# The first mixture's products in three fp32r parts, with split weights kept in DRAM and two smaller weight rings

## What is computed

```python
def _expert(xf, w1, w3, w2):
    return jax.nn.silu(xf @ w1) * (xf @ w3) @ w2
# D = 256, H = 128; routed_w1, routed_w3: (8, D, H), routed_w2: (8, H, D); shared_w*: the same for 2
```

## Time and profile before

| | us |
|---|---|
| median of 3 runs | 4491.06 (4484.61 to 4496.41) |
| the profiled execution, its own time | 4493.15 |
| its span, first to last instruction | 4491.3 |
| TensorE busy | 4192.4 (93%) |
| VectorE busy | 2936.4 (65%) |
| ScalarE busy | 2086.3 (46%) |
| mean granted TensorE clock | 0.973 of full |
| DRAM traffic | 202.34 MB read, 20.97 MB written |

### The profile page before, as it was taken

How to read it: one execution, slowest core, us unless ns; L and a number is a source line. 1 busy time by engine, 2 the same in 40 slices (tenths; PEclk the granted TensorE clock), 3 DMA queues, 4 the chain that set the end, 5 groups by cost and what they waited for, 6 DMA issues and landing times.

```text
span 4491.3 us, 73765 instructions
## 1 busy us (share of the span) xinstructions
PE 4192.4 (93%) x28256; PEld 3197.8 (71%) x28256; DVE 2936.4 (65%) x7633; ACT 2086.3 (46%) x3424; POOL 112.0 (2%) x196
## 2 busy tenths in 40 slices
PE   7898998989989899898999989999999999999998
PEld 4675966759667596675966759667696676956768
DVE  7567776676656666666665667657676576665655
ACT  4544455353553435535355353553535535356342
POOL 0000000000000000000000000000000000000000
PEclk8999999999999999999999999999999999999999
DMA  2010600103001030010300103001030010300112
GB/s 99 1 45 10 219 35 1 54 20 132 29 15 41 27 125 29 15 41 29 123 29 15 41 29 123 29 15 41 29 123 29 15 41 37 115 29 15 31 54 102
DMA packets 51768, 228.05 MB, mean 51 GB/s; under 512 B 4832, under 2 KB 21216, under 8 KB 31584
## 3 DMA queue, kind: packets, MB, share of 16 engines
q1 hardware_dynamic: 51424, 223.33, 13.8%
HBM read 202.34 MB, written 20.97 MB: 50 GB/s over the span
## 4 chain that ended last, share of the span: by engine, by line
PE 81%; DVE 11%; ACT 5%; issue 3%; DMA 0%; SPq 0%; DVEq 0%; ACTq 0%
PE w L574 18%; PE w L584 13%; PE o L709 11%; PE w L830 8%; PE w L820 8%; PE w L642 4%; PE w L558 4%; PE o L702 3%; DVE mx L1227 3%; PE w L625 3%; PE w L677 2%; PE w L567 2%; PE w L721 1%; PE w L612 1%; ACT pt_spread L975 1%
## 5 line engine op out<-in xcount | busy, mean ns | idle before, releaser
L1227 DVE TENSOR_REDUCE mx<-w 128x4 f32<-128x1024 f32 x512 | 606.8, 1221 | 181.4 <-PE w L625 168.4
L975 ACT ACTIVATE pt_spread<-w 128x1024 f32<-128x1024 f32 x512 | 520.2, 1024 | 235.5 <-PE w L642 202.9
L709 PE MATMUL o<-pt_spread,va 128*32 128x256 f32 x4096 | 540.9, 395 | 29.3 <-ACT pt_spread L975 28.6
L921 ACT ACTIVATE oth<-w,res 128x256 f32<-128x256 f32 x656 | 277.4, 472 | 574.6 <-PE w L820 469.8
L574 PE MATMUL w<-xnT,stream 128*128 128x256 f32 x1792 | 413.1, 382 | 1.4 <-ACT xnT L913 0.8
L574 PEld LDWEIGHTS w<-xnT,stream 128*128 128x128 f32 x1792 | 338.1, 191 | 50.8 <-DVE x L1196 1.0
L709 PEld LDWEIGHTS o<-pt_spread,va 128*32 128x32 f32 x4096 | 204.8, 111 | 200.0 <-issue 60.8
L820 PE MATMUL w<-qodd,va_hi 128*128 128x256 f32 x2048 | 344.9, 283 | 0.9 <-issue 0.6
L820 PEld LDWEIGHTS w<-qodd,va_hi 128*128 128x128 f32 x2048 | 284.6, 188 | 7.6 <-issue 2.3
L1483 DVE TENSOR_REDUCE mx<-w 128x2 f32<-128x1024 f32 x128 | 155.8, 1225 | 199.6 <-PE w L679 199.1
L1196 DVE SCALAR_TENSOR_TENSOR x<-w,gate,x 128x256 f32<-128x256 f32 x512 | 223.2, 477 | 89.8 <-PE w L830 71.7
(11 more groups left out here) (255 smaller groups left out, 7741.9 us busy)
## 6 DMA issues: line engine op xcount, KB each, us to landing
stream_lo<-split SPq DMA_DIRECT2D x56, 1024.0 KB, 4.8
va_hi<-split SPq DMA_DIRECT2D x56, 1024.0 KB, 6.9
stream<-in_moe_dram SPq DMA_DIRECT2D x80, 384.0 KB, 3.2
stream<-in_resident_dram SPq DMA_DIRECT2D x8, 2048.0 KB, 7.4
raw<-in_moe_dram SPq DMA_DIRECT2D x8, 1024.0 KB, 6.8
split<-va_hi SPq DMA_DIRECT2D x8, 1024.0 KB, 8.9
split<-stream_lo SPq DMA_DIRECT2D x8, 1024.0 KB, 10.9
stream<-in_resident_dram SPq DMA_DIRECT2D x8, 1024.0 KB, 4.7
```

The source lines that it names most:

```text
L709: mm = pe.matmul(o[g:g + 32, 0:T], by_heads(plan, s)[:, kt, plan.v_of(h), :], p[:, a * 512 + kt * T:a * 512 + (kt + 1) * T], start=(kt == ...
L921: h = act.activation(dst[:, c, :], w[:, c * T:(c + 1) * T], func, bias=bias[:, c:c + 1], **more)
L975: act.activation(exp_buffer(plan.name + ".exp", s, u), w[:, :], ACT.Exp, scale=scale).then_inc(S["s_P"], 1)
L1227: dve.tensor_reduce(mx[s][:, :, 2 * v:2 * v + 2].rearrange("p t a -> p a t"), w[:, :].rearrange("p (a t k) -> p a t k", a=2, t=TT), AX_X, ...
```

## The change

**Products.** f1's products become three fp32r products each. `f1.up` waits for the split activations of the element (`f1.xs`, new: VectorE copies `xnT` to a high part in `qodd` and subtracts for the low part) and issues 12 instead of 4; `f1.down` issues 6 instead of 2. The hidden activations are split too: after `f1.mul` ScalarE copies the product to a high part, and a new step `f1.part` on VectorE subtracts it for the low part; both lie in `ob_hi`.

**Weights.** In the first pass each expert's raw weights are loaded into the place of the low part and split by a new step `f1.split` (ScalarE: two copies, 512 and 256 columns; VectorE: two subtractions). SP writes both parts to DRAM (`split_up1`, `split_down1`), and in the seven later passes loads them split. Split weights take twice the room, so the ring of five becomes a ring of three for the up weights (1024 columns each, 512 KB) and a ring of two for the down weights (512 columns each, 256 KB): `RINGU`, `RINGD`. A load waits for both slots' `f1.up` of e-3 or `f1.down` of e-2, and in the first pass also for the write of what lay there. The loads of f2's first low parts wait for the last uses of the new regions.

**Order.** The new steps are put in, and the string `ORDER` is another one, so steps that the change doesn't name stand in another order as well.

```diff
 MOE1, MOE1_ROUTED, MOE1_COLS = 10, 8, 2 * 128 + 2 * 128 + 256
-RING1, RING2 = STREAM_COLS // MOE1_COLS, 2
+UP1_COLS, DOWN1_COLS = 2 * 512, 2 * 256
+RINGU, RINGD, RING2 = 3, 2, 2
+DOWN1_AT = RINGU * UP1_COLS
...
@@ -173,7 +175,7 @@
 def experts(n, s, count):
-    return [(f"{n}.{what}", s, e) for e in range(count) for what in ("up", "mul" if n == "f1" else "part", "down", "sum")]
+    return [(f"{n}.{what}", s, e) for e in range(count) for what in (("up", "mul", "part", "down", "sum") if n == "f1" else ("up", "part", "down", "sum"))]
...
@@ -184,7 +186,7 @@
-        + steps_of(s, "l2.init", "l1.oT", "l1.out", "f1.ln", "f1.xT", "f1.lg", "f1.gate") + experts("f1", s, MOE1)
+        + steps_of(s, "l2.init", "l1.oT", "l1.out", "f1.ln", "f1.xT", "f1.xs", "f1.lg", "f1.gate") + experts("f1", s, MOE1)
...
@@ -226,52 +228,54 @@
-        + [[x for x in every if x[0] == "l1.max"] + [("f2.split", s, e) for e in range(MOE2) if s == 0]]
+        + [[x for x in every if x[0] == "l1.max"] + [("f1.split", s, e) for e in range(MOE1) if s == 0] + [("f2.split", s, e) for e in range(MOE2) if s == 0]]
...
 ORDER = (
...
-    "DAM11ADM11ADDAAMAAAA7AAAJAMAAAAAAAMA1AMMAMAD0M050M50M505M0M50M50M50M5M0550M50M50M5M0M505M0M55CC5HC0HCHCHCHCHC2H0CH0CHHC0"
...
+    "DAM11ADM11ADDAAMAAAA7AAAJAMAAAAAAAMA1AMMAMAD0M050M50M505M0M50M50M50M5M0550M50M50M5MM0505M0M55CC5HCHCHCHCH0CHCHCH0CH0H0CH"
...
+        split_up1 = nc.dram_tensor("split_up1", (MOE1, P, UP1_COLS), F32, kind="Internal").ap()
+        split_down1 = nc.dram_tensor("split_down1", (MOE1, P, DOWN1_COLS), F32, kind="Internal").ap()
...
 
-        def expert1(e):
-            w = stream[:, e % RING1 * MOE1_COLS:(e % RING1 + 1) * MOE1_COLS]
-            return (w[:, 0:256].rearrange("p (k n) -> p k n", k=FC), w[:, 256:512].rearrange("p (k n) -> p k n", k=FC),
-                    w[:, 512:768].rearrange("p (k n) -> p k n", k=1))
+        def up1(e, buf):
+
+            w = buf[:, e % RINGU * UP1_COLS:(e % RINGU + 1) * UP1_COLS]
+            return w[:, 0:512], w[:, 512:1024]
+
+        def down1(e, buf):
+            o = DOWN1_AT + e % RINGD * DOWN1_COLS
+            return buf[:, o:o + 256], buf[:, o + 256:o + 512]
+
+        def loads1(p, e, ring):
+
...
@@ -771,18 +787,34 @@
 
             def ffn_1(what, s, e):
-                w1, w3, w2 = expert1(e)
                 w = take("f1." + what, s, e)
                 if what == "lg":
                     pe.wait_ge(*after("s_xnT", "f1.xT", s))
                     filled(by_tokens(w, xnT[s], mat("r1_w", FC), 8, FC))
                 elif what == "up":
-                    pe.wait_ge(S[f"s_moe1_{e % RING1}"], 16 * (pass_of(s) * len(range(e % RING1, MOE1, RING1)) + e // RING1 + 1))
-                    by_features(w, w1, xnT[s], 0, 1)
-                    filled(by_features(w, w3, xnT[s], 0, 1, T))
+                    if pass_of(s):
+                        pe.wait_ge(S[f"s_moe1_{e % RINGU}"], loads1(pass_of(s), e, RINGU))
+                    else:
+                        pe.wait_ge(*after("s_wl1", "f1.split", 0, e))
+                    pe.wait_ge(*after("s_xs", "f1.xs", s))
+                    hi, lo = (p.rearrange("p (j k n) -> p j k n", j=2, k=FC) for p in up1(e, stream_lo))
+                    xhi, xlo = qodd[s][:, 0:2, :], qodd[s][:, 2:4, :]
+                    for j in range(2):
+                        parts = [(wt, a, k) for wt, a in ((hi, xhi), (lo, xhi), (hi, xlo)) for k in range(FC)]
+                        for n, (wt, a, k) in enumerate(parts):
+                            mm = pe.matmul(w[:, j * T:(j + 1) * T], wt[:, j, k, :], a[:, k, :], start=(n == 0), stop=(n == len(parts) - 1))
+                    filled(mm)
                 else:
-                    pe.wait_ge(*after("s_up1", "f1.mul", s, e))
-                    filled(by_tokens(w, oth[s][:, 2 * (e % 2) + 1:2 * (e % 2) + 2, :], w2, D, 1))
+                    if pass_of(s):
+                        pe.wait_ge(S[f"s_moed_{e % RINGD}"], loads1(pass_of(s), e, RINGD))
+                    pe.wait_ge(*after("s_up1", "f1.part", s, e))
+                    hi, lo = down1(e, stream_lo)
+                    ahi, alo = (ob_hi[s][:, 2 * (e % 2) + n, :] for n in range(2))
+                    for tt in range(TT):
+                        parts = ((ahi, hi), (alo, hi), (ahi, lo))
+                        for n, (a, wt) in enumerate(parts):
+                            mm = pe.matmul(w[:, tt * D:(tt + 1) * D], a[:, tt * P:(tt + 1) * P], wt, start=(n == 0), stop=(n == len(parts) - 1))
+                    filled(mm)
...
@@ -1076,9 +1108,19 @@
                     w = full(act, step, s, u)
                     if u > 1:
-                        act.wait_ge(*after("s_up1", "f1.mul", s, u - 2))
+                        act.wait_ge(*after("s_mul", "f1.mul", s, u - 2))
                     act.activation(oth[s][:, 2 * (u % 2), :], w[:, 0:T], ACT.Silu).then_inc(S["s_silu"], 1)
 
+                elif step == "f1.mul":
+                    if u > 1:
+                        full(act, "f1.down", s, u - 2)
+                    act.wait_ge(*after("s_mul", step, s, u))
+                    act.activation(ob_hi[s][:, 2 * (u % 2), :], oth[s][:, 2 * (u % 2) + 1, :], ACT.Copy).then_inc(S["s_h1hi"], 1)
+                elif step == "f1.split":
+                    act.wait_ge(S[f"s_moe1_{u % RINGU}"], loads1(0, u, RINGU))
+                    act.wait_ge(S[f"s_moed_{u % RINGD}"], loads1(0, u, RINGD))
+                    act.activation(up1(u, stream_lo)[0], up1(u, stream)[1], ACT.Copy)
+                    act.activation(down1(u, stream_lo)[0], down1(u, stream)[1], ACT.Copy).then_inc(S["s_wh1"], 1)
                 elif step == "f2.split":
                     if u < 2:
...
@@ -1495,8 +1537,18 @@
                     w = full(dve, "f1.up", s, u)
                     dve.wait_ge(*after("s_silu", "f1.up", s, u))
                     if u > 1:
+                        dve.wait_ge(*after("s_h1hi", step, s, u - 2))
+                    dve.tensor_tensor(oth[s][:, 2 * (u % 2) + 1, :], w[:, T:2 * T], oth[s][:, 2 * (u % 2), :], ALU.mult).then_inc(S["s_mul"], 1)
+                elif step == "f1.part":
+                    dve.wait_ge(*after("s_h1hi", "f1.mul", s, u))
+                    if u > 1:
                         full(dve, "f1.down", s, u - 2)
-                    dve.tensor_tensor(oth[s][:, 2 * (u % 2) + 1, :], w[:, T:2 * T], oth[s][:, 2 * (u % 2), :], ALU.mult).then_inc(S["s_up1"], 1)
+                    hi, lo = (ob_hi[s][:, 2 * (u % 2) + n, :] for n in range(2))
+                    dve.tensor_tensor(lo, oth[s][:, 2 * (u % 2) + 1, :], hi.bitcast(F32), ALU.subtract).then_inc(S["s_up1"], 1)
+                elif step == "f1.split":
+                    dve.wait_ge(*after("s_wh1", step, s, u))
+                    dve.tensor_tensor(up1(u, stream_lo)[1], up1(u, stream)[1], up1(u, stream_lo)[0].bitcast(F32), ALU.subtract)
+                    dve.tensor_tensor(down1(u, stream_lo)[1], down1(u, stream)[1], down1(u, stream_lo)[0].bitcast(F32), ALU.subtract).then_inc(S["s_wl1"], 1)
                 elif step == "f1.sum":
...
-
-                    dve.wait_ge(*after("s_mla", "f2.mla", s))
+                elif step in ("f1.xs", "f2.xs"):
+
+                    dve.wait_ge(*(after("s_xnT", "f1.xT", s) if stage == "f1" else after("s_mla", "f2.mla", s)))
                     link(dve.tensor_copy(qodd[s][:, 0:2, :], xnT[s][:, :, :]))
                     dve.tensor_tensor(qodd[s][:, 2:4, :], xnT[s][:, :, :], qodd[s][:, 0:2, :].bitcast(F32), ALU.subtract)\
                        .then_inc(S["s_xs"], 1)
...
+                def load_up1(e):
+                    if e >= RINGU:
+                        used("f1.up", e - RINGU)
+                    elif e < 2:
+                        for step in ("l1.kc", "l1.vc", "l1.kl", "l1.vl"):
+                            used(step, 0)
+                    else:
+                        used("l1.q", 0)
+                    n = e % RINGU
+                    if p:
+                        sp.dma_start(stream_lo[:, n * UP1_COLS:(n + 1) * UP1_COLS].bitcast(F32), split_up1[e]).then_inc(S[f"s_moe1_{n}"], 16)
+                        return
+                    if e >= RINGU:
+                        sp.wait_ge(s_kept_up1[n], 16 * (e // RINGU))
+                    sp.dma_start(up1(e, stream)[1], moe1_in[e][:, 0:512]).then_inc(S[f"s_moe1_{n}"], 16)
+
+                def load_down1(e):
+                    if e >= RINGD:
+                        used("f1.down", e - RINGD)
+                    else:
+                        used("l1.out", 0)
+                    n, o = e % RINGD, DOWN1_AT + e % RINGD * DOWN1_COLS
+                    if p:
+                        sp.dma_start(stream_lo[:, o:o + DOWN1_COLS].bitcast(F32), split_down1[e]).then_inc(S[f"s_moed_{n}"], 16)
+                        return
+                    if e >= RINGD:
+                        sp.wait_ge(s_kept_down1[n], 16 * (e // RINGD))
```

(38 more changed lines are left out.)

96 lines of the change are left out of this document (53 added, 43 removed), and 4 rows, old and new, of tables (READ, SIGNALS).

## The result

The changed kernel takes 4564.72 us (median of 3 runs, 4559.60 to 4566.62) against 4491.06 us: 1.62% slower (ratio 1.0162, 95% interval 1.0137 to 1.0188), so 73 us more. The forecast was 4507 us with a range of 4445 to 4540. The sign of the likeliest case was right, the size was not, and the time lies outside the range. A second set of five runs gave 4562.88 us (1.0169, 1.0155 to 1.0183).

A forecast was written before the change was run, and what follows sets the result against it. It took TensorE's rate to bound the kernel inside the mixture and VectorE around it. Terms -74+36+6+24+12+12 = +16 on 4493 gave 4509, less 2.1 for the profile 4507 us; range 4445 to 4540.

The forecast's parts named there:

- the likeliest case: The forecast itself, chance 0.40: TensorE's gain is handed back in waits for VectorE and splits, 4507 us, so slower.
- Rate, -74: First mixture's products: three fp32r products replace one fp32 product, saving TensorE 9.2 us a pass, 74 us in all.
- VectorE, 10.6 us more a pass: In each pass's mixture VectorE gets 10.6 us more from subtracting low parts and splitting activations.
- Head, +36+6: Start of the mixture, passes 2 to 8: TensorE idles before f1.xT of slot 1, +36 us; waits right behind, +6.
- that path from up to down: Between an expert's up and down: four steps, 2.2 us, taken as covered by other TensorE work and costed at nothing.
- Ends, +24: Around l1.back and l1.oT, and at the mixture's tail: TensorE lacks cover, 3.4 us in each of seven passes, +24 us.
- First pass, +12+12: First pass, which splits the weights: late start of f1.up 0, +12 us; refill, split and write of experts, +12 us.
- Idle time together: TensorE's added waits at head, ends and first pass taken together: 90 us.
- The clock: TensorE's granted clock: no loss in the forecast's sum; drops behind new idle gaps were left to a rival.
- rival (c): New TensorE gaps of 4 to 7 us drop the clock, adding 32 us: 4539 us; chance 0.15.

The follow-up runs named there:

- nosplit_2: The changed kernel without splitting of the first mixture's weights or writing of split parts; every pass loads both parts from DRAM: 4545.96 us, ratio 1.0134.
- the run with the gap: The kernel before, with ten throwaway VectorE additions ahead of f1.ln of slot 1 in every pass: 4578.16 us, ratio 1.0197.
- gapfill: The kernel before, with the same VectorE delay plus eleven throwaway fp32 products before the wait of f1.xT of slot 1: 4566.93 us, ratio 1.0179.

## Why the prediction was wrong

The sum was -74+36+6+24+12+12 = +16 us; the span of the profile moved by +66.5.

- **Rate, -74.** The products are 0.118 us apart as forecast: in the fourth pass twelve, twenty-four and thirty-six in a row take 1.66, 3.08 and 4.51 us at the full clock. In one order they free 68.6 us of TensorE; 44 to 54 of them reach the time. Right within a tenth in work, and the loss of cover was not in the sum.
- **VectorE, 10.6 us more a pass.** In the mixtures' windows it is 49.67-39.76 = 9.9 us, the first pass's splits included; over the whole span of nosplit_2, which has the new steps and no splits, it is (3013.4-2936.4)/8 = 9.6 us. Right within a tenth.
- **Head, +36+6.** The mechanism is as forecast, a chain of 10.6 us with too little cover: in full in passes 2, 5, 6 and 8, where the whole wait is that of f1.xT, and in part in passes 4 and 7, where f1.xT waits 2.15 and 2.49 us. The waits are 5.27, 3.4, 4.9, 4.4, 4.4, 4.7 and 5.3 us, with what stands right behind or ahead of f1.xT, 32 us in all: over-sized by 10. In the third pass f1.xT waits for nothing: the 2.63 us stand ahead of it, where f1.down 0 waits for f1.part, which is queued on VectorE behind l1.out. The prediction cost that path from up to down at nothing. What the order of steps did not show is that in the fourth pass f1.down 0 waits 2.79 us for its weights, whose load starts only when l1.out of both slots has left that memory.
- **Ends, +24.** Outside the mixtures and behind the start of the first there are 14 us more idle time, and in the mixtures of passes 2 to 8 another 10 that do not stand at the heads; which of these are the ends was not told apart. Head and ends together were forecast at 66 us and measured at 57.
- **First pass, +12+12.** 25 us measured, right by accident. Two terms of it share one piece of time: the wait for the splits and the wait for f1.xT both stand behind the same VectorE chain, and I left the second out for this pass. The splits' own part is 7 us of idle time.
- **Idle time together: forecast 90, measured 82 us.** This half of the working held.
- **The clock: forecast nothing, measured 58 us.** This is the step that failed. I gave it to rival (c) with a chance of 0.15 and priced it at 32 us, as if a gap of 4 to 7 us dropped the clock once or twice in the mixture only. The trace has 131 us more at the half level, about half of it in the mixtures (63 us by the clocks of their windows) and half outside them. At 0.37 to 0.42 us each (the runs above) that is 48 to 55 of the 58. The argument against (c), that VectorE would hide a slower TensorE behind the gap, is refuted: with the gap filled the kernel is 22 to 26 us faster.
- **The order elsewhere.** I read the order at the head and the ends only. Of the 111 us that the order costs in fp32, about 31 are not there.

The rule of the Trainium skill on gaps above about 3 us, cited beside (c), named the missing term, and I gave it too small a chance. Its 3 us are not a safe bound here either, since the clock also fell behind gaps of 2.63 and 2.79 us. At the ratio of the run with the gap (85 for 50) the 90 us of idle time would have come to 153 with their clock loss; measured are 82+58 = 140.

## What to carry to other kernels

In this kernel idle gaps of TensorE of 6.4 to 7.4 us cost about 1.7 times the idle time they added (85 us for 50), since the products behind it run at half the clock: price a gap with its clock, and look for it first where TensorE was fully busy. A change that needs smaller buffers can be paid for in the order of the steps, as here, so count the cover that the old order had and the new one can't have, and remember that faster products cover less. Throwaway products are a quick test of whether the clock is the cost, and good cover only where their PSUM bank is free and they reach nearly to the end of the gap.

## What the hardware showed that I had not expected

Ten microseconds at a granted clock of 0.51 follow a gap of 5.27 us, though TensorE is then busy for 9.25 of them. How long the gap was did not by itself tell what followed: 2.63 and 2.79 us were followed by the half level, two gaps of 2.17 and 2.49 us were not, and behind the fill in gapfill 1.80 us were and 1.92 us were not. And the drop is not tied to the place of the change: about 68 of the 131 us more at the half level lie outside the mixtures, where the idle time grew by 25 us.
